# Attention sums from a 33rd column of v, halved transposes, reordered projections, and finished rows turned by transposing transfers

## What is computed

```
q = Wq @ layernorm(x) + bq ; k = Wk @ ctx + bk ; v = Wv @ ctx + bv     # per batch: 128 channels x 1024 positions
dots[h,t,w] = q[h,:,t] . k[h,:,t-8+w] * 16**-0.5      # 8 heads of 16 channels, a window of 16 positions
attn = softmax(dots over w)
out[h,:,t] = sum_w attn[h,t,w] * v[h,:,t-8+w]
x = x + tanh(g_xattn) * (Wo @ out + bo)
x = x + tanh(g_ffn) * (silu(n @ G) * (n @ U)) @ D,  n = layernorm(x)
```

## Time and profile before

| | us |
|---|---|
| median of 3 runs | 1631.78 |
| the runs | 1631.67, 1631.78, 1643.83 |
| the profiled execution's own time | 1639.15 |
| its span | 1636.9 |

### The profile page before, as it was taken

The page is one execution under the profiler, slowest core; times in us unless marked ns, Lnnn a source line. Parts: engine busy times, 40 slices in busy tenths (PEclk is TensorE's granted clock), DMA queues, the critical chain, the costliest instruction groups (busy, mean ns, idle before and its releaser), DMA issues.

```text
span 1636.9 us, 40533 instructions
## 1 busy us (share of the span) xinstructions
PE 1556.0 (95%) x16614; PEld 811.9 (50%) x16614; DVE 1450.1 (89%) x1425; ACT 1054.3 (64%) x1191; POOL 1256.5 (77%) x925
## 2 busy tenths in 40 slices
PE   5899999898789999999999999999999999999996
PEld 3566666666434444444444444444444444444444
DVE  4688877777598999999999999999999999999997
ACT  4577777777566666666666666666666666666652
POOL 4576776666546888888888888888888888888865
PEclk9899999999899999999999999999999999999999
DMA  4666665645434666666666666676666676667569
GB/s 121 161 149 147 172 150 139 156 125 140 128 117 114 148 152 153 152 153 152 152 152 155 154 154 155 153 154 147 153 152 153 146 155 156 151 154 155 116 180 321
DMA packets 192274, 249.50 MB, mean 152 GB/s; under 512 B 14446, under 2 KB 138030, under 8 KB 192074
## 3 DMA queue, kind: packets, MB, share of 16 engines
q1 hardware_dynamic: 168186, 163.74, 35.3%
q0 software_dynamic: 22752, 82.85, 28.8%
q10 hardware_dynamic: 1152, 0.33, 0.1%
HBM read 113.92 MB, written 16.78 MB: 80 GB/s over the span
## 4 chain that ended last, share of the span: by engine, by line
PE 90%; issue 4%; SPq 2%; POOL 1%; DVE 1%; DMA 1%; ACT 1%; ACTq 0%; DVEq 0%; POOLq 0%
PE bank L1182 69%; PE bank L1091 3%; PE bank L1080 3%; PE bank L1123 2%; PE bank L1043 2%; PE bank L1054 2%; PE bank L1039 2%; PE bank L1047 2%; PE bank L1101 1%; PE bank L1070 1%; PE bank L1051 1%; PE bank L1059 1%; POOL oacc L620 1%; SPq L396 1%; DMA gates<-in_g_ffn_dram 1%
## 5 line engine op out<-in xcount | busy, mean ns | idle before, releaser
L969 DVE SCALAR_TENSOR_TENSOR acc<-bank,scale,acc 128x1024 f32<-128x1024 f32 x784 | 969.6, 1279 | 52.0 <-PE bank L1182 15.1
L1182 PE MATMUL bank<-xT,w_int 128*128 128x512 f16 x3584 | 846.4, 379 | 7.5 <-DVE xT L920 3.7
L620 POOL TENSOR_TENSOR oacc<-oacc,d_part 128x1024 f32<-128x1024 f32 x219 | 536.7, 2455 | 54.0 <-ACT d_part L806 48.7
L1182 PEld LDWEIGHTS bank<-xT,w_int 128*128 128x128 f16 x3584 | 349.9, 98 | 431.6 <-DVE xT L920 5.3
L806 ACT ACTIVATE d_part<-bank,scale 128x1024 f32<-128x1024 f32 x219 | 244.1, 1115 | 200.9 <-PE bank L1182 197.0
L1182 PE MATMUL bank<-h_hi,d_int 128*128 128x512 f16 x896 | 339.6, 379 | 2.1 <-ACT d_part L806 1.8
L1182 PE MATMUL bank<-h_lo,d_int 128*128 128x512 f16 x896 | 339.6, 379 | 0.0
L806 ACT ACTIVATE d_more<-bank,scale 128x1024 f32<-128x1024 f32 x158 | 176.3, 1116 | 154.5 <-PE bank L1182 154.5
L564 POOL TENSOR_TENSOR raw_z<-raw_w,raw_z 128x512 int32<-128x512 int32 x168 | 225.6, 1343 | 19.1 <-DMA raw_z<-in_L_ffn_gate_z_dram 11.1
L622 POOL DMA_DIRECT2D oacc<-d_more x158 | 150.2, 951 | 114.1 <-ACT d_more L806 107.8
L610 POOL TENSOR_TENSOR h_lo<-acc,h_hi 128x1024 f16<-128x1024 f32 x56 | 129.5, 2312 | 23.1 <-ACT h_hi L788 23.1
(11 more groups left out here) (86 smaller groups left out, 1530.1 us busy)
## 6 DMA issues: line engine op xcount, KB each, us to landing
oacc<-d_more POOLq DMA_DIRECT2D x158, 512.0 KB, 5.2
raw_w<-in_L_ffn_gate_w_dram SPq DMA_DIRECT2D x56, 256.0 KB, 3.4
raw_z<-in_L_ffn_gate_z_dram SPq DMA_DIRECT2D x56, 256.0 KB, 4.2
raw_w<-in_L_ffn_up_w_dram SPq DMA_DIRECT2D x56, 256.0 KB, 3.4
raw_z<-in_L_ffn_up_z_dram SPq DMA_DIRECT2D x56, 256.0 KB, 4.0
raw_w<-in_L_ffn_down_w_dram SPq DMA_DIRECT2D x56, 256.0 KB, 2.9
raw_z<-in_L_ffn_down_z_dram SPq DMA_DIRECT2D x56, 256.0 KB, 3.7
vt<-vn_hl SPq DMA_DIRECT2D x64, 192.0 KB
```

The lines of the kernel that those rows point to most:

```text
L620: nc.gpsimd.tensor_tensor(into, into, d_part[:, (n - 1) % 2, :], ALU.add).then_inc(d_added, 1)
L969: nc.vector.scalar_tensor_tensor(out=into, in0=pair[u % 4][:, :, :].rearrange("p h r -> p (h r)"), scalar=scale[:, par, i, m, k:k + 1], in ...
L1182: last = nc.tensor.matmul(dst[:, h, :], weights, rows_of(h, part), start=(part == 0), stop=(part == 1))
```

## The change

- **Sums.** v on partitions (`vn_hl`, `vt`, `v_pad`) gets a 33rd column of ones behind each head's 16 high and 16 low columns. `mix` multiplies 33 columns, each head in its own 64 columns of two PSUM banks, and column 33 is the sum. `add_up` and its ones are gone; the reciprocal moves into `take_mix`.
- **Mask matmuls.** Each of the two now uses its own 64 rows of `spread` and `window` in place of all 128.
- **Halved transposes.** `turn_probs(n, hg)` and `take_pT(n, hg)` do one half of 8 at a time, both through one bank: the first half at the end of step n+1, the second in step n+2 behind that step's first tasks. `mix` now comes behind all tasks of its step.
- **Order of tasks.** k; v and t; q and t; o. The `x` tasks are gone. `norm_x` writes two halves and moves from step 0 to the end of step 1 on ACT, with its moments split over steps 0 and 1; the moments of the finished row are split over steps 1 and 2; the residual is added in two halves.
- **Finished rows.** `norm_row` writes the row already scaled; ACT writes its fp16 high part into a new buffer `x_hl` (`high_row`, step 3), POOL writes the low part in two halves (`low_row`, steps 0 and 1 of the next batch), and SP issues two transposing transfers of 128 by 1024 fp16 from `x_hl` into `xT` (`turn_rows`). They stand behind the transfers of v and ahead of the load of x. The first feed-forward unit waits for the rows of batches 0 to 7, unit 48 and ACT's first take of a down product for all.
- **Start.** Half of batch 0's k transfers are issued by ACT; the first normalization no longer stands behind the load of the gates; PE's first projections no longer wait for the masks; the transposes of the scales come after the first scores.

```diff
@@ tasks and their order
-            x = [("x", b - 2, 0)] if b >= 2 else []
-            x_end = [("x", b - 3, 1)] if b >= 3 else []
-            return ((x_end, k[:1], k[1:]), (q[:1], q[1:], t[:1]), (v[:1], v[1:], t[1:]), (x, o[:1], o[1:]))[s]
+            return ((k[:1], [], k[1:]), (v[:1], v[1:], t[:1]), (q[:1], q[1:], t[1:]), (o[:1], o[1:], []))[s]
@@ SP
+            def turn_rows(b):
+
+                sp.wait_ge(x_hi, b + 1)
+                sp.wait_ge(x_lo, 2 * b + 2)
+                if b >= B - 2:
+                    sp.wait_ge(projected, done("o", B - 1, 1))
+                for part in range(2):
+                    sp.dma_start_transpose(out=xT[:, b, part], in_=x_hl[:, part, :]).then_inc(x_turned, 16)
...
                 if b + 2 < B:
-                    load_x(b + 2)
                     load_ctx(b + 2)
                 if b + 1 < B:
                     place_v(b + 1)
+                if b >= 3:
+                    turn_rows(b - 3)
+                if b + 2 < B:
+                    load_x(b + 2)
@@ POOL
+            def low_row(b, n):
+
+                pool.wait_ge(x_hi, b + 1)
+                half = slice(n * HALF, (n + 1) * HALF)
+                nc.gpsimd.tensor_tensor(x_hl[:, 1, half], xr[:, half], x_hl[:, 0, half], ALU.subtract).then_inc(x_lo, 1)
...
-                    if s == 2:
-                        set_residual(b)
                     split_p(b, s)
+                    if s < 2 and b >= 3:
+                        low_row(b - 3, s)
+                    if s >= 2:
+                        set_residual(b, s - 2)
@@ ACT
+            def high_row(b):
+                act.wait_ge(row_normed, b + 1)
+                if b:
+                    act.wait_ge(x_turned, 32 * b)
+                nc.scalar.activation(x_hl[:, 0, :], xr[:, :], ACT.Copy).then_inc(x_hi, 1)
...
                     for t in first:
                         take_high(*t)
+                    if n >= 2:
+                        take_pT(n - 2, 1)
+                    for t in second:
+                        take_high(*t)
                     exp(n)
-                    for t in second + third:
+                    for t in third:
                         take_high(*t)
                     if n:
-                        take_pT(n - 1)
-                    if s == 1 and b >= 2:
+                        take_pT(n - 1, 0)
+                    if s == 1 and b + 1 < B:
+                        norm_x(b + 1)
+                    if s == 2 and b >= 2:
                         norm_row(b - 2)
+                    if s == 3 and b >= 2:
+                        high_row(b - 2)
@@ PE
-                    if n >= 3:
-                        add_up(n - 3)
                     scores(b, s)
                     first, second, third = tasks_of(b, s)
-                    for t in first + second:
+                    for t in first:
+                        project(*t)
+                    if n >= 2:
+                        turn_probs(n - 2, 1)
+                    for t in second + third:
                         project(*t)
                     if n >= 2:
                         mix(n - 2)
-                    for t in third:
-                        project(*t)
...
-                        turn_probs(n - 1)
+                        turn_probs(n - 1, 0)
```

More of the change, by code:

```diff
@@ L393, in move_k @@
                 for h in range(HG):
-                    for hg in range(2):
+                    for hg in halves:
                         lo = GC * hg + HD * h
@@ L577, in _ @@
[L577 to L582 removed]
+            made = 1
@@ L605, in _ @@
             normalize(S * B - 1)
+            for n in range(2):
+                low_row(B - 3, n)
             def low_hidden(c, q):
@@ L627, in one @@
                         take_zero(*at)
+                    if first and u in (NEXT_LOW, LAST_LOW):
+                        for n in range(2):
+                            low_row(B - 2 if u == NEXT_LOW else B - 1, n)
                     if first and u == LAST_STD:
@@ L742, in _ @@
                     n = S * b + s
-                    if s == 0 and b + 1 < B:
-                        norm_x(b + 1)
                     first, second, third = tasks_of(b, s)
@@ L845, in _, with moments, moments_x @@
         def _(dve):
-            def moments(b, which, s_stats, s_mv):
-                for n in range(2):
+            def moments(b, which, s_stats, s_mv, halves):
+                for n in halves:
                     nc.vector.bn_stats(out=stats[:, which, n, :], in_=rows[b % 4][:, n * HALF:(n + 1) * HALF])\
                         .then_inc(s_stats, 1)
-                dve.wait_ge(s_stats, 2 * b + 2)
-                nc.vector.bn_aggr(out=mv[:, which, :], in_=stats[:, which, :, :]).then_inc(s_mv, 1)
-            def moments_x(b):
+                if halves[-1]:
+                    dve.wait_ge(s_stats, 2 * b + 2)
+                    nc.vector.bn_aggr(out=mv[:, which, :], in_=stats[:, which, :, :]).then_inc(s_mv, 1)
+            def moments_x(b, halves=(0, 1)):
                 dve.wait_ge(x_loaded[b % 2], 16 * (b // 2 + 1))
@@ L862, in moments_row @@
                     dve.wait_ge(shift2_done, b)
-                moments(b, 1, stats2_done, mv2_done)
+                moments(b, 1, stats2_done, mv2_done, halves)
             def soften(b, s):
@@ L917, in take_low @@
                                                    op0=ALU.add, op1=ALU.subtract).then_inc(emptied_proj, 1)
-                elif kind == "x":
-                    hi, lo = (xT[:, b, part, 4 * n:4 * n + 4, :].rearrange("p k r -> p (k r)") for part in range(2))
-                    nc.vector.scalar_tensor_tensor(out=lo, in0=src, scalar=XS, in1=hi,
-                                                   op0=ALU.mult, op1=ALU.subtract).then_inc(emptied_proj, 1)
             moments_x(0)
@@ L938, in _ @@
                     soften(b, s)
+                    if s == 1 and 0 < b < B - 1:
+                        moments_x(b + 1, (1,))
+                    if s == 2 and b >= 2:
+                        moments_row(b - 2, (1,))
                     first, second, third = tasks_of(b, s)
-                    for t in first:
+                    for t in first + second:
                         take_low(*t)
```

304 lines of the change are left out of this document (148 added, 156 removed).

## The result

The changed kernel takes 1688.61 us (median of 4 runs, 1686.05 to 1691.47) against 1632.19 before (4 runs, 1631.67 to 1643.83). The ratio is 1.0337, with a 95% interval of 1.0299 to 1.0375. The prediction said 1594, range 1575 to 1625: the sign was wrong.

A forecast was written before the change was run, and what follows sets the result against it. The prediction took PE's work as the bound: 19.2 us of work, 1.8 of waits and 2.0 of holes make 23.0 a batch for 25.16. Savings of 28 + 2.4 + 6 + 2 = 38 us off the median 1631.78 gave 1594, range 1575 to 1625.

The forecast's parts named there:

- the sum: Whole kernel: 38 us off, of which 28 from batches 3 to 15 at 23.0 us each in place of 25.16.
- What bounds the kernel before: Attention: PE's own work is the limit; it can lose about 3 us a batch before another engine sets the pace.
- PE's parts: PE per batch: add_up 1.6 us, x tasks 1.0 and masks 0.6 saved, transposes unchanged at 0.89; work falls to 19.2.
- The other engines: Work per attention batch: DVE 18.4 us, ACT 18.4, POOL 19.5, with POOL the fullest.
- The waits of the new order: Attention: waits added by halved transposes and moved tasks, 1.8 us a batch, bounds 0 and 4.
- q's wait for `norm_x`: Step 2: q of the next batch waits for norm_x's first half on ACT; part of the 1.8 us.
- The holes: PE's idle gaps with releaser issue: 2.0 us a batch in place of 2.8, bounds 1 and 4.
- The clock: PE's granted clock, 1.00 in a full batch: named as a risk if PE pauses, with no price in the sum.
- SP and T: SP's queue: T, one transposing transfer, takes 2.0 us; the queue needs 20.4 us a batch, hidden behind 23.0.
- The rival on the other side: SP's queue becomes the bound: T = 6.2 us per transposing transfer, 28.8 us a batch, 1669 us; chance 0.13.
- The start: Kernel start: gates off the path and k's issues split gain 6 us (bounds 0 and 8); batches 1 and 2 gain 2.4.
- The end: First feed-forward units: DVE loses four low parts, 2.6 us, but ACT's first take waits for the last row; 2 us gained.

The follow-up runs named there:

- e6: Changed kernel with a second buffer for the split rows, odd rows below 13 going to a still unused part of xT: 1669.52 us, ratio 1.0194.
- e3: Changed kernel with the two transposing transfers of a batch ahead of v's transfers in SP's queue: 1663.18 us, ratio 1.0183.
- e5: Changed kernel with the finished rows undone: x tasks back on PE, no x_hl and no transposing transfers: 1644.04 us, ratio 1.0061 to the kernel before.
- e7: e5 with the x task last in step 3 and the second half transposes ahead of q in step 2: 1627.44 us, ratio 0.9965.
- after: The changed kernel with the whole change, against the kernel before it: 1688.61 us, ratio 1.0337.
- e2: Changed kernel with each transposing transfer replaced by a plain copy of the same bytes at the same place in the queue: 1680.11 us, ratio 1.0259.
- before: The kernel without the change, the reference of the ratios: 1632.19 us.
- e9: e7 with mix ahead of the step's last task and, in step 0, the first k task behind the second half transposes: 1619.31 us, ratio 0.9919.
- e8: Changed kernel without transposing transfers for batches 0 to 13 and, from batch 2 on, without the transfers placing k and v: 1614.19 us, ratio 0.9883.
- e10: Changed kernel whole with one edit, mix ahead of the step's last task: 1702.36 us, ratio 1.0434.
- e4: Changed kernel with each mask matmul issued four times, some 32 us of added PE work: 1680.89 us, ratio 1.0291.

## Why the prediction was wrong

On the spans, the sum was off by 90.5 us: 38.4 were to be gained and 52.1 were lost. From the start of batch 3 (100.37 before, 101.98 after) to the first feed-forward unit 41.7 us were lost where 28 were forecast to be gained; batches 0 to 2 lost 1.6 in place of gaining 8.4; the part behind lost 8.8 in place of gaining 2. In the steady batches, 28.2 us in place of 23.0, the 5.2 are 2.5 of clock, 1.8 of holes, 0.7 of work and 0.2 of waits; the experiments say that a wait that the prediction left out stands behind a good part of them.

- **What bounds the kernel before:** right, PE. That its work could shrink by 3 us before another engine sets the pace was wrong in kind: of the 22.4 + 2.8 us the 2.8 was a second limit, by my reading the instruction blocks, which less work does not lift.
- **PE's parts:** the masks' saving (0.15 a step) and the end of add_up and x tasks came as summed; 64 matmuls of mix take 0.60 (246.77 to 247.37) with the 33rd column, as with 32 before. The 16 transposes do not take 0.89 in two runs as in one: a half ahead of the masks takes 0.55 (204.89 to 205.44), one ahead of a projection 0.45 (201.91 to 202.36), together 0.4 a batch more. Work is 19.9 for 19.2; the rest of the 0.7 was not looked for.
- **The other engines:** DVE 19.0 and ACT 18.9 for 18.4, POOL 19.7 for 19.5. Right, and none is the bound.
- **The waits of the new order, 1.8 us: 2.0 measured,** and the nearness of the two is luck. q's wait for `norm_x`, which was named, is 0.8 of it. Mix waiting for `pT` is 1.1, named at some tenths and for another reason; with ACT's wait gone (e6) it is 0.3. **The step that failed first is here:** the list of waits went through task order and halves, and left out `high_row`'s wait on `x_turned`, although the diff shows it. On the time it is worth 19 us (e6) to 25 (e3).
- **The holes, 2.0 us: 3.8 measured,** at the upper bound of 4. That PE issues fewer matmuls did not bring them down. That part of a hole falls into a wait is borne out by e5 and e7, but the steady batches of the changed kernel have waits and more holes. Holes come where a block is run through fast and its successor's packet is late; density was no term of the sum.
- **The clock, 0 us: 2.5 measured.** It stood last among the things that would make the sum wrong, without a price. It should have been a term. How much idle time there is does not tell it: e5 is idle for 40.5 us with no gap over 1.61 and a granted clock of 1.00, after for 54.1 with seven gaps over 2 us and 0.92.
- **SP and T:** T = 2.0 was a choice between 0.37 and 6.2 and came out right, 4.07 for two in the mean; in e3's place in the queue two take 2.8. SP keeps gaps of 5.7 to 7.9 us a batch; DVE never waits for x in the stretch. The rival on the other side, SP as the bound, did not happen: the slower outcome came by ACT, for which there was no rival. Of the Trainium skill's two pages, the 1309 ns a block of "VectorE: DVE Perf Modes" can't be multiplied up to a whole row: that gave an estimated 10.5 us, and a transfer holds SP's queue for 2.0 and lands 5.0 after its issue (medians over the kernel for landing). By "Advanced Engine Details and Errata", X-Bar Transpose (TRN2), they are as fast as regular ones: in landing e2 agrees (5.6 us for its plain copies), in the time of SP's queue it does not, 4.07 us for two against 1.5.
- **The start, 6 us and 2.4 for batches 1 and 2:** the first masks are at 21.69, 3.0 us earlier and not 6; PE waits for DVE's low halves instead (3.27 and 1.08 us). Even the 3.0 are no gain, since the transposes of the scales now stand behind the first scores: the masks of step 1 come at 31.16, before at 28.37. Batch 2 starts 0.5 us earlier than before, batch 3 1.6 later.

```profile
14.61 2.07 PE L1096 MATMUL bank<-xn,wq 128*128 128x512 f32 x2 [3.27 <-DVE k_hl L967]
19.47 2.08 PE L1088 MATMUL bank<-wv,ct 128*128 128x128 f32 x8 [1.08 <-DVE q_hl L971]
21.69 0.50 PE L1115 MATMUL bank<-window,spread 64*128 64x384 bf16 x2
...
23.54 3.16 PE L1178 MATMUL bank<-ident,xT 16*128 16x16 f32 x28
```

- **The end, 2 us gained: 8.8 lost.** The sum looked only at the last row. POOL, ACT and PE in the fourth feed-forward unit:

```profile
484.14 2.28 POOL L557 TENSOR_TENSOR x_hl<-xr,x_hl 128x512 f16<-128x512 f32 x2
486.38 2.50 POOL L584 TENSOR_TENSOR raw_z<-raw_w,raw_z 128x512 int32<-128x512 int32 x2
```

```profile
487.68 0.63 ACT L746 ACTIVATE w_int<-raw_z 128x512 f16<-128x512 int32 x1 [4.53 <-POOL raw_z L584]
...
491.05 1.06 ACT L732 ACTIVATE x_hl<-xr 128x1024 f16<-128x1024 f32 x1 [1.60 <-DMA xT<-x_hl]
492.01 0.58 ACT L685 ACTIVATE xT<-bank 128x512 f32<-128x512 f32 x1
```

```profile
492.64 3.60 PE L1217 MATMUL bank<-xT,w_int 128*128 128x512 f16 x8 [5.04 <-ACT xT L685]
```

The low halves of a row (2.28 us) stand on POOL ahead of the weights' subtraction, ACT's cast waits for that, `high_row` then waits 1.60 us for the transfer of the row before, and only behind it ACT takes t's half, for which PE has waited 5.04 us. With the rows back on PE nothing is lost there: from the first feed-forward unit to the end it is 1201.4 us in e5 and 1201.6 in before, against 1210.4 in after.

Undone one after the other (by medians of different groups), the time goes from 1688.6 through e5's 1644.0 (rows back on PE), e7's 1627.4 (two waits for ACT) to e9's 1619.3 (mix ahead of the last task). e9's batch of 23.3 us is about the 23.0 forecast, with the x tasks' 1.0 us of work still in it: the sums, the masks and the new order come near it without the rows' part. Its time of 1619.3 is still 25 above the forecast.

What stays open: why the holes grew, and why a block's packet at times starts 4 to 6.6 us after the block before it was entered. The DMA share does not order the kernels (median 1.3 us in e8 with 0.21, 1.5 in e9 with 0.70, 1.9 in after).

## What to carry to other kernels

When an edit moves work to a transfer, list every wait that the diff adds and ask what stands behind the waiting instruction on its in-order engine; a single buffer whose release is last in a queue cost this kernel 19 to 25 of the 33 us that the transfers cost in all. When PE's work shrinks, price its pauses too: the clock and the instruction supply are limits of their own, and in e9 short matmuls did better set between long ones, as long as nothing made mix wait (e10). When a hole is put down to "issue", count the engine's instructions up to it.

## What the hardware showed

- PE's instructions come in packets of 16,384 bytes, one for each 256 instructions, which the profile counts among those of the core's 16 DMA engines; in before PE goes on 1.2 to 1.7 us after a late one landed. All of this is from counted records; no record shows the wait itself. At such places lay all of PE's idle time in the steady attention of the kernel before, 22.1 us in 251.6.
- More work on PE need not cost time: 32 us of filler, and 8 us less (e4, two runs; the intervals overlap a little).
- Idle time of PE does not by itself lower the clock: 40.5 us idle in 251.6 at a granted 1.00 in e5, 22.2 us at 0.98 in before, where the longest gap is 3.59.
- Two 128x1024 fp16 transposing transfers between buffers of SBUF hold SP's queue for 3.3 to 5.0 us in the attention of after, 2.6 to 3.3 ahead of v's transfers (e3), and plain copies in their place 1.2 to 2.4 (e2), which changes the time by 8 us of 1688.
